# The second layer's expert list made in three parts instead of two, its pieces multiplied in one go, and its blocks put two steps apart

## The reference, cut to what matters

```
x = x + L0_attn(layernorm(x))
x = x + L0_ffn(layernorm(x))
x = x + L1_attn(layernorm(x))            # |q - k| <= 128
logits  = layernorm(x) @ Wg + bg
one_hot = one_hot(argmax(logits), 8)
h = gelu(einsum('td,edh->eth', xf, W1))  # 256 -> 1024
y = einsum('eth,ehd->etd', h, W2)        # 1024 -> 256
x = x + einsum('etd,te->td', y, one_hot)
```

## Time and profile before

| | |
|---|---|
| time, median of 3 runs | 1512.81 us (1508.42 to 1516.38) |
| time of the profiled execution | 1514.26 us |
| its span in the profile | 1512.5 us |
| mean granted TensorE clock | 0.966 of full |
| PE matmuls busy | 1417.0 us (94%) |
| DVE, ACT, POOL busy | 691.5, 478.4, 446.3 us |
| chain that ended last | PE 78%, DVE 7%, DMA 5%, ACT 3%, issue 4% |

### The profile page before, as it was taken

The page is one execution under the profiler, slowest core; times in us unless marked ns, Lnnn a source line. Parts: engine busy times, 40 slices in busy tenths (PEclk is TensorE's granted clock), DMA queues, the critical chain, the costliest instruction groups (busy, mean ns, idle before and its releaser), DMA issues.

```text
span 1512.5 us, 23794 instructions
## 1 busy us (share of the span) xinstructions
PE 1417.0 (94%) x7759; PEld 1048.9 (69%) x7759; DVE 691.5 (46%) x2451; ACT 478.4 (32%) x925; POOL 446.3 (30%) x533
## 2 busy tenths in 40 slices
PE   6899999999999999989989999999998998899998
PEld 4666655567777777645666666666665797899998
DVE  5643346523333333335778787878686122200000
ACT  1211111011221112111567665665655412111211
POOL 1100000035222222241454453544323323334432
PEclk9898999999999999999999999999998799999999
DMA  9400100011111212122454454435441577799996
GB/s 334 120 29 15 56 0 1 3 42 62 60 63 63 64 58 62 52 90 76 122 157 136 128 156 151 140 106 163 133 133 57 194 260 261 267 346 333 342 345 223
DMA packets 88582, 204.28 MB, mean 135 GB/s; under 512 B 11373, under 2 KB 45295, under 8 KB 78480
## 3 DMA queue, kind: packets, MB, share of 16 engines
q1 hardware_dynamic: 72512, 167.99, 33.3%
q0 software_dynamic: 12096, 32.13, 7.3%
q10 hardware_dynamic: 3856, 2.64, 0.6%
HBM read 151.48 MB, written 52.17 MB: 135 GB/s over the span
## 4 chain that ended last, share of the span: by engine, by line
PE 78%; DVE 7%; DMA 5%; issue 4%; ACT 3%; SPq 2%; POOL 0%; DVEq 0%; POOLq 0%; ACTq 0%
PE psum L737 12%; PE psum L619 10%; PE psum L907 9%; PE psum L917 8%; PE psum L716 6%; PE psum L630 5%; PE psum L763 4%; DMA qT<-strips 4%; PE psum L810 4%; PE psum L785 3%; PE psum L834 3%; PE psum L863 2%; PE psum L546 2%; PE psum L698 2%; DVE work L1732 2%
## 5 line engine op out<-in xcount | busy, mean ns | idle before, releaser
L1732 DVE CUSTOM_DVE_ANT_0 work<-psum,mask 128x384 bf16<-128x384 f32 (+1 forms) x512 | 230.9, 485 | 96.0 <-PE psum L763 94.1
L763 PE MATMUL psum<-kz,qT 96*128 96x384 f32 (+1 forms) x512 | 174.2, 408 | 24.5 <-DVE small L1732 14.8
L737 PE MATMUL psum<-arena,work 128*128 x568 | 187.4, 473 | 2.8 <-ACT work L1054 2.4
L1808 POOL DMA_INDIRECT work<-normed,token_of x71 | 67.4, 949 | 349.4 <-PE psum L698 210.2
L619 PE MATMUL psum<-arena 128*128 128x512 f32 x320 | 153.6, 626 | 0.0
L907 PE MATMUL psum<-arena 128*128 128x128 f32 x1248 | 149.4, 279 | 1.2 <-issue 1.2
L907 PEld LDWEIGHTS psum<-arena 128*128 128x128 f32 x1248 | 146.1, 196 | 1.7 <-issue 1.7
L763 PEld LDWEIGHTS psum<-kz,qT 96*128 96x128 f32 x512 | 92.1, 198 | 78.3 <-DVE small L1732 42.3
L1135 ACT ACTIVATE arena<-psum 128x384 f32<-128x384 f32 x256 | 112.3, 494 | 99.0 <-PE psum L785 98.1
L917 PE MATMUL psum<-arena 128*128 128x256 f32 x624 | 141.1, 380 | 0.0
L737 PEld LDWEIGHTS psum<-arena,work 128*128 128x128 f32 x568 | 103.1, 191 | 54.2 <-issue 5.6
(11 more groups left out here) (223 smaller groups left out, 2048.8 us busy)
## 6 DMA issues: line engine op xcount, KB each, us to landing
arena<-in_w SPq DMA_DIRECT2D x78, 1024.0 KB
strips<-hi SPq DMA_DIRECT2D x64, 256.0 KB
kz<-strips SPq DMA_DIRECT2D x64, 192.0 KB, 3.8
qT<-strips SPq DMA_DIRECT2D x32, 384.0 KB, 5.3
results<-work SPq DMA_DIRECT2D x71, 128.0 KB, 1.7
strips<-lo SPq DMA_DIRECT2D x32, 256.0 KB
normed<-work SPq DMA_DIRECT2D x14, 512.0 KB, 3.2
X<-in_x SPq DMA_DIRECT2D x8, 512.0 KB, 10.1
```

The costliest lines, as they stand in the source:

```text
L737: m = e.matmul(psum[:, pair[u], 0:INTER], xsT0[:, b % 2, c * P:(c + 1) * P], wu0[:, bass.ds(x, 1), c, u * INTER:(u + 1) * INTER], start=(c ...
L763: m = e.matmul(psum[:, bk, at:at + w], qT[0:ROWS_S, slot, half, i * P:(i + 1) * P], kz[slot][0:ROWS_S, hd, lo_key:hi_key], start=True, sto ...
L1732: e.tensor_tensor_reduce(masked[:, n % 2, 0:w], psum[:, bank_of["scores", u, i, hd], at:at + w], mask[:, P - off:P - off + w], 1.0, MASKED ...
L1808: e.indirect_dma_start(out=xs[:, b % 3, :], out_offset=None, in_=normed[l][0:n, :], in_offset=bass.IndirectOffsetOnAxis(ap=token_of[:, l, ...
```

## The change: three lists, pieces in one go, blocks two steps apart

Three things change. The list of the late blocks is cut in two: blocks 12 to 19, which tokens of batches 0 to 6 always fill, get a list of their own after batch 6, whose gate moves from step 146 to 142; blocks 20 to 38 are listed after batch 7 as before. DVE makes each list's pieces into eight separate buffers, and PE multiplies all pieces of a list in one go (`pe_list`), where it took each a step after it was made, with two buffers. The one-hot rows `one_r` are kept from list to list, so that only new batches' are made. And all 39 blocks get one table, two steps apart from step 130.

```diff
-EARLY_B = 5
-EARLY = (EARLY_B * N - NX * (P - 1)) // P
-GATE_AT = [PRE * b + (46 if b in (EARLY_B - 1, B - 1) else 50) for b in range(B)]
+LIST_B = (5, 7, B)
+LIST_END = [(n * N - NX * (P - 1)) // P for n in LIST_B[:2]] + [NBLK1]
+LIST_FIRST = [0] + LIST_END[:2]
+LIST_N = [end - first for first, end in zip(LIST_FIRST, LIST_END)]
+GATE_AT = [PRE * b + (46 if b + 1 in LIST_B else 50) for b in range(B)]
...
-for b in (B - 2, B - 1):
+for b in range(B - 3, B):
     PICK_AT[b], RANKS_AT[b], PLACES_AT[b] = [GATE_AT[b] + 1], GATE_AT[b] + 2, [GATE_AT[b] + 3]
...
-ROWS_AT = [130, 131, 134, 137, 140, 143, 146, 150, 154, 159, 161, 163]
-UP_AT = ROWS_AT[1:] + [165]
-DOWN_AT = [135, 138, 141, 144, 147, 152, 156, 160, 162, 164, 166, 168]
-LATE_AT = LISTED_AT[1] + 9
-ROWS_AT += [LATE_AT - 1] + [LATE_AT + 2 * k for k in range(NBLK1 - EARLY - 1)]
-UP_AT += [LATE_AT + 2 * k for k in range(NBLK1 - EARLY)]
-DOWN_AT += [LATE_AT + 2 * k + 3 for k in range(NBLK1 - EARLY)]
...
+PIECES_AT = [[LISTED_AT[0] + 1 + n for n in range(LIST_B[0] * TPB // CH)]]
+PIECES_AT += [[LISTED_AT[i] + 1 + n // 2 for n in range(LIST_B[i] * TPB // CH)] for i in (1, 2)]
+FOUND_AT = [at[-1] + 2 for at in PIECES_AT]
+ROWS_AT = [130 + 2 * k for k in range(NBLK1)]
+UP_AT = [at + 1 for at in ROWS_AT]
+DOWN_AT = [at + 4 for at in ROWS_AT]
+FETCH_AT = [FOUND_AT[0] + k for k in range(3)] + [at - 4 for at in ROWS_AT[3:]]
+for i in (1, 2):
+    FETCH_AT[LIST_FIRST[i]:LIST_END[i]] = [max(at, FOUND_AT[i]) for at in FETCH_AT[LIST_FIRST[i]:LIST_END[i]]]
...
-            return (0, 1) if u in (0, *LIST_UNITS) else (0, 1, 2)
+            return (0, 1) if u == 0 else (0, 1, 2)
...
+        def pe_list(e, i, ring):
+            w, pieces = 3 * LIST_N[i], len(PIECES_AT[i])
+            bk = next_of(ring)
+            fill(e, ("list", i), bk)
+            for n in range(pieces):
+                e.wait_ge(ones_made, sum(map(len, PIECES_AT[:i])) + n + 1)
+                for t in range(CH):
+                    m = e.matmul(psum[:, bk, 0:w], one_r[n][:, t, :], one_b[n].rearrange("p t k b -> p t (k b)")[:, t, 0:w],
+                                 start=(n == 0 and t == 0), stop=(n == pieces - 1 and t == CH - 1))
+            m.then_inc(bank_full[bk], 1)
...
+            if n >= (0, *LIST_B)[i]:
+                e.tensor_tensor(one_r[n], repeat(count[:, :]), spread(places[:, 0, ts], P), ALU.is_equal).then_inc(rows_hot, 1)
```

More of the change, by code:

```diff
@@ L144, in blocks_at, with list_of, piece @@
     return [k for k in range(NBLK1) if at[k] + behind == step]
-def piece(step, behind=0):
-    return [(i, n) for i in range(2) for n, at in enumerate(PIECES_AT[i]) if at + behind == step]
+def list_of(k):
+    return [i for i in range(3) if LIST_FIRST[i] <= k < LIST_END[i]][0]
+def piece(step):
+    return [(i, n) for i in range(3) for n, at in enumerate(PIECES_AT[i]) if at == step]
 def later(step, behind=0):
@@ L300, in build @@
         which = carve(work, 4512 + NB1 * NX, NB1)
[L301 to L304, removed]
+        one_r = [carve(arena, 6144 + i * CH * P // 2, CH * P // 2).bitcast(BF16)
+                 .rearrange("p (t r) -> p t r", t=CH) for i in range(NT // CH)]
+        one_b = [carve(work, 4512 + NB1 * (NX + 1) + i * CH * 3 * NB1 // 2, CH * 3 * NB1 // 2).bitcast(BF16)
+                 .rearrange("p (t k b) -> p t k b", t=CH, k=3) for i in range(NT // CH)]
+        assert 4512 + NB1 * (NX + 1) + NT // CH * CH * 3 * NB1 // 2 <= 5632
         xn = carve(work, 0, 2, TPB, E)
@@ L951, in pe_attention @@
                                 pe_ranks(e, b, ring)
-                        for i, n in piece(s, 1):
-                            pe_list_piece(e, i, n)
+                        for i in range(3):
+                            if s == FOUND_AT[i] - 1:
+                                pe_list(e, i, ring)
                         for b, _ in batch(s, 28):
@@ L1481, in dve_no_tokens @@
             e.memset(max_parts[:, :, :, :].bitcast(F32), 0.0)
+            e.memset(taken, 0.0)
             e.memset(chosen[:, :, 0:1], 0.0)
@@ L1527, in dve_list @@
         def dve_list(e, i):
-            n, first = (EARLY, NBLK1 - EARLY)[i], (0, EARLY)[i]
+            n, first = LIST_N[i], LIST_FIRST[i]
             yield from dve_link(e, e.tensor_scalar(n_int, n_int, P.bit_length() - 1, None, ALU.arith_shift_right))
             yield from dve_link(e, e.tensor_copy(n_blocks, n_int))
[L1533 to L1537, removed]
+            yield from dve_link(e, e.tensor_tensor(left_now, n_blocks, taken, ALU.subtract))
+            yield from dve_link(e, e.tensor_tensor_scan(up_to, ones[:, 0:NX], left_now, 0.0, ALU.mult, ALU.add))
             e.tensor_tensor(offset, n_blocks, up_to, ALU.subtract)
@@ L1564, in dve_list_piece @@
                 e.wait_ge(list_set, i + 1)
-                e.wait_ge(placed, (EARLY_B, B)[i])
-            if m >= 2:
-                e.wait_ge(ones_read, m - 1 if i == 0 else max(m - 2, len(PIECES_AT[0]) - 1))
-            e.tensor_tensor(one_r[m % 2], repeat(count[:, :]), spread(places[:, 0, ts], P), ALU.is_equal)
+                e.wait_ge(placed, LIST_B[i])
+                if i == 0:
+                    for k in range(2):
+                        e.wait_ge(strips_kept[k], 16 * KEPT * EC * B)
+                else:
+                    e.wait_ge(*done["list", i - 1])
+            if n >= (0, *LIST_B)[i]:
+                e.tensor_tensor(one_r[n], repeat(count[:, :]), spread(places[:, 0, ts], P), ALU.is_equal).then_inc(rows_hot, 1)
             e.tensor_tensor(one, repeat(block_row[:, 0:w]), spread(places[:, 1, ts], w), ALU.is_equal).then_inc(one_hot_made, 1)
+            e.wait_ge(rows_hot, max(n + 1, (0, *LIST_B)[i]))
             e.wait_ge(one_hot_made, m + 1)
@@ L1574, in dve_tokens @@
         def dve_tokens(e, i):
-            n, first = (EARLY, NBLK1 - EARLY)[i], (0, EARLY)[i]
-            tile_no, row, one = (psum[:, LIST_BANK[i], k * n:(k + 1) * n] for k in range(3))
+            n, first = LIST_N[i], LIST_FIRST[i]
+            tile_no, row, one = (psum[:, bank_of["list", i], k * n:(k + 1) * n] for k in range(3))
             f = [found[k][:, 0:n] for k in range(2)]
@@ L1636, in dve_attention @@
                     dve_result(e, k)
-                for i in range(2):
-                    if s == PIECES_AT[i][-1] + 2:
+                for i in range(3):
+                    if s == FOUND_AT[i]:
                         dve_tokens(e, i)
@@ L1896, in pool_rows1 @@
         def pool_rows1(e, k):
-            if k in (0, EARLY):
-                e.wait_ge(tokens_listed, 1 if k == 0 else 2)
-                for b in range(EARLY_B) if k == 0 else range(EARLY_B, B):
+            if k in LIST_FIRST:
+                i = list_of(k)
+                e.wait_ge(tokens_listed, i + 1)
+                for b in range((0, *LIST_B)[i], LIST_B[i]):
                     e.wait_ge(tokens_kept[b], 16 * 2)
@@ L1960, in sp_first_weights @@
         def sp_first_weights(e, k):
-            if k in (0, EARLY):
-                e.wait_ge(experts_listed, 1 if k == 0 else 2)
+            if k in LIST_FIRST:
+                e.wait_ge(experts_listed, list_of(k) + 1)
             if k == 0:
```

36 lines of the change are left out of this document (17 added, 19 removed).

## The result

| | before | change |
|---|---|---|
| median of the first comparison | 1510.62 us (4 runs) | 1489.76 us (1484.67 to 1492.24, 4 runs) |
| ratio | | 0.9862, 95% interval 0.9822 to 0.9902 |
| second comparison, on one chip | 1509.1 us (25 runs) | 1488.91 us (6 runs), ratio 0.9877 (0.9842 to 0.9911) |
| mean of all runs | 1510.0 us (49 runs, deviation 5.3) | 1488.9 us (11 runs, deviation 2.9) |
| profiled execution, its span | 1514.26, 1512.5 us | 1484.67, 1482.9 us |

The change is faster by 1.2 to 1.4%, about 21 us. I had forecast 1499 us within 1491 to 1508, 13.7 us less than before. The direction was right; the time lies 1.2 us under the range.

What follows compares the result with a forecast made beforehand. PE was taken as the bound, transfers close behind. Removed waits 11.2 and slow matmuls 3.1, plus 1.0 for the third bank, less 1.6 for added pieces, made 13.7 us: forecast 1499 us, range 1491 to 1508.

Steps and rivals of the forecast that it cites:

- R(8)'s wait: PE's wait of 6.96 us before R(8), for its gather; forecast to go.
- the seam's three: PE's waits before R(12), R(13) and U(13), of 2.70, 0.53 and 1.05 us; forecast to go.
- the gather behind batch 7's scale: Block 11's gather, to start about 8.2 us after D(6) and land at 16.6; PE work before R(11) 19.8.
- The 0.86 before batch 6's transposes: PE's wait of 0.86 us for a PSUM bank that DVE reads; forecast to stay.
- The additional table loads: Two more ACT loads in the attention's tail; forecast covered by 1.1 us, costing nothing, or 2.6 us if uncovered.
- Slow matmuls removed: Two U partly at the lower clock, 5.20 and 5.36 us against 3.74; forecast gain 3.1 us.
- 28 more matmuls of pieces: PE multiplies seven more list pieces; forecast cost 1.6 us.
- The third bank: Third score bank for units 30 and 31, against PE's 1.46 us wait for DVE; forecast gain 1.0 us.
- Late gather: Rival: row gather late at block 11, 12 or 20; PE waits 2.6 us at both lists, 1507 us; chance 0.13.
- The lower clock elsewhere: Rival: the slow stretch from 1172 us goes or stays elsewhere; 4.5 us gained, 1494.5, or lost; chance 0.13.
- The attention's tail: Rival: a wait from the loads and U(1), 2.6 us and a slow stretch, 1502 to 1503 us; chance 0.05.
- Weights: Rival: weight transfers fall behind, deciding from 320 GB/s down; 15 us lost there, slower below; chance 0.07.

Runs made afterwards that it cites:

- e3: Kernel of before with its twelve early blocks two steps apart and no middle list: 1522.66 us (8 runs), ratio 1.0099.
- e7: Changed kernel with the gathers of blocks 12 to 14 at step 155 and of 20 to 22 at 171: 1506.13 us (10 runs), ratio 0.9963.
- e5: Changed kernel with U(1) at step 134, behind the last pass of unit 31: 1487.09 us (6 runs), ratio 0.9864.
- e4: Changed kernel with two score banks for units 30 and 31, as before: 1494.66 us (12 runs).
- e12: Second trace of the changed kernel with two score banks for units 30 and 31: 1497.37 us.
- e2: Changed kernel with the block table of before (twelve early blocks three steps apart), keeping lists, buffers and third bank: 1499.53 us (12 runs), ratio 0.995.
- e6: Changed kernel with U(0) to U(2), D(0) and D(1) moved so no gelu precedes an exponential: 1492.28 us (6 runs), ratio 0.9875.
- e8: Changed kernel with an additional, never read load of half of W2 (0.52 MB) for each of blocks 12 to 38: 1504.98 us (one run).

## Why the prediction was wrong, point by point

**Holes and their cover: right.** R(8)'s wait, the seam's three and the slow U behind them are gone. (The two D that stand together before the seam, 7.14 us, are D(10) and D(11), not D(9) and D(10); the times read from them are right.) The working for the gather behind batch 7's scale said 8.2 us from D(6)'s end; POOL's timeline has it:

```profile
1251.92 1.02 POOL L1819 DMA_INDIRECT arena<-normed,token_of  x1 [0.46 <-issue]
```

D(6) ends at about 1243.9, so 8.0. From D(8)'s end at 1260.9 to the gather of block 12 it is 2.0, as taken from before:

```profile
1262.84 0.98 POOL L1819 DMA_INDIRECT arena<-normed,token_of  x1 [5.96 <-DVE token_out L1601]
```

PE reached R(11) 20.5 us after D(6)'s end, against 19.8 in the working. e3 and e7 show from the other side that these covers are what pays: taken away, 15 us slower than before and 17 slower than the change.

**What stays: right.** The 0.86 before batch 6's transposes is there as 0.87. The additional table loads cost nothing that can be told (e5), and each took 1.28 us with the exponential right behind, as in the earlier trace rows:

```profile
1187.28 1.28 ACT L1141 ACT_TABLE_LOAD   x1
1188.57 0.60 ACT L1141 ACTIVATE arena<-psum 128x512 f32<-128x512 f32 x1
```

So the Trainium skill's price of 2.66 us for a switch (ScalarE: Activation LUTs, What ACT_TABLE_LOAD costs) does not hold for this pair: the load alone is what the traces show, with no drain before or behind it.

**The sum: 3.5 us too small; this is the first step that failed.** Forecast for the stretch from unit 27 on: 13.7. Measured: 17.2. Ahead of U(0), where only the bank counts, 2.0 were gained for a forecast 1.0. Behind U(0) it was 15.1 for 12.7. There the removed waits were sized about right: 11.2 forecast, 10.4 measured. What was too small is the gain in PE's busy time: 3.1 us of slow matmuls less 1.6 for the added pieces make 1.5, and 4.7 were measured. The terms:

- *Slow matmuls removed, 3.1 us.* I read them from one trace, the one with the longest wait before R(8) and the least loss behind it. The second trace of before has a shorter wait and a slower U(7):

```profile
1260.49 0.66 PE L698 MATMUL psum<-ident,arena 128*128 128x128 f32 x2 [5.16 <-DMA arena<-normed,token_of]
1260.94 6.09 PE L907 MATMUL psum<-arena 128*128 128x128 f32 x32
```

  By U(7) and U(12) the three traces lost 3.1, 4.7 and 4.6 us, 4.1 in the mean: 1.0 of the error.

- *28 more matmuls of pieces, priced 1.6 us.* The price took the shown length of a group, which holds more than the group's delay to what follows. The 80 matmuls of the change show 2.6 us in all; in PE's timeline the 28 of the middle list delay the next R by 0.71 us (1256.46 to 1257.17):

```profile
1256.46 0.86 PE L897 MATMUL psum<-work,arena 128*128 128x24 bf16 x28
1257.17 0.42 PE L705 MATMUL psum<-ident,arena 128*128 128x128 f32 x2
```

  and taking a list in one go saves the gaps of the small groups (0.26 beside others in the list of before). This term was near 0.5 by my estimate, so 1.1 of the error.
- *The third bank, 1.0:* 2.0 by the traces of before and change, 2.8 by e4 and e12: 1.0 or more of the error. The slow U(1), which I had not foreseen, took nothing from it in two of the change's three traces (U(0) to the end of U(2) as above); in the third it is 27.9 us.
- *The rest,* about 1 us of busy time behind U(0), and the 0.8 by which the waits were put too high, are not separated.

DVE, which I called idle four fifths of the stretch from 1200 to 1310, was idle 72% of it; nothing hung on it.

**The base: 2.8 us too high; the second step that failed.** I set the sum against the median of three runs, 1512.81. Over 49 runs before has a mean of 1510.0 and a deviation of 5.3; three runs say little about it. The range had the uncertain terms in it and not this scatter. With the right base and the right stretch the forecast is 1510.0 - 17.2 = 1492.8. Either correction alone would have put 1489.8 inside a range of the same width.

**What is left, 4 us,** lies ahead of unit 27. From the means, less the 1.7 by which a time exceeds its span, before's common part is 1510.0 - 1.7 - 379.8 = 1128.5 us and the change's 1488.9 - 1.7 - 362.6 = 1124.6. The same reckoning gives 1125.1 for e3 (before's code there, 8 runs). With the change's code there it gives 1125.1 for e2, 1123.3 for e5, 1125.6 for e7, 1128.6 for e4 with e12 and 1129.3 for e6 (12, 6, 10, 13 and 6 runs). That looks like scatter, since it falls on both sides, but it takes one or two traces' stretch for the mean of many runs, and a small effect of the changed program on the rest isn't excluded. It stays open.

**The rivals.** Late gather: did not occur; e7, where it was forced, prices it at 8 us for each seam, twice my figure: the waits were 5.6 and 6.4 us and not 2.6, and what stands behind them lost 2.5 us to the lower clock and not 1.5. The lower clock elsewhere: neither gained nor lost; the slow stretch of the earlier trace rows stayed (3.42 us for the gate's matmuls again), and the one around the exponentials moved onto U(1). The attention's tail: no wait before the values of unit 31. Weights: the pace stayed at 7.24 us; the threshold of 320 GB/s was set on the belief that a busy share of 96% is a full queue, and e8 moved 399.

## What to carry to other kernels

Before a row of dependent small steps (ranks, list, gather), count the bulk work that the bound engine has left in program order; if a part of the list can be closed earlier because its entries are certain, split it, and the bulk work behind it becomes cover. Packing the same bulk work more densely without adding any takes the cover away: it cost 16.9 us here (e3), where the lists alone gained 5.5 (e2) and both together 17.2. And set a forecast against the scatter of many runs: where the common part of two kernels wanders by 15 us, a pair of spans says nothing about a change of 15, while a stage cut out by two events that both kernels have repeats within 3.

## What the runs showed of the hardware that I had not expected

- The same program differs by 22 us between executions (1498.3 to 1520.25 us, 49 runs), and the granted clock follows it: 0.972 in the fastest, 0.959 in the slowest.
- A wait of 5 to 7 us on PE cost 1.5 to 2.6 us more in the matmuls behind it, which run partly at 1.2 GHz: 5.20 for 3.74 us after 6.96 in the first trace of before, 6.09 after 5.16 in the second, 6.13 and 6.24 for 3.62 after 5.63 and 6.40 in e7. The longer wait was not the dearer one.
- The DMA engines can be 96% busy at 340 GB/s and still give 399 when more is asked (e8).
- A gather of 128 rows of 1 KB took 5.8 and 6.4 us from the start of its issue among the weight loads (e7), 3.9 to 4.1 at before's seam, and 6.6 to 8.4 beside the stores of batch 7.
